# Key parts, score maxima and value biases of a two-layer attention kernel moved between engines and DMA queues

## The reference

```python
x = x + attention0(norm(x), ctx)   # 16 heads of 8, keys and values from ctx, biases bq bk bv bo
x = x + butterfly_ffn(norm(x))     # 128 -> 512 by W_exp and 9 butterfly stages, gelu, 9 stages and W_con back
x = x + attention1(norm(x), ctx)   # the same shape, its own weights
x = x + experts(norm(x))           # sigmoid router, top 4 of 16 experts of width 64, one shared expert
```

## Time and profile before

| | us |
|---|---|
| median of 3 runs | 208.7 |
| the profiled execution | 208.64 |
| its span in the trace | 206.8 |
| PE busy | 197.8 (96%) |
| DVE busy | 151.3 (73%) |
| ACT busy | 146.4 (71%) |
| POOL busy | 57.7 (28%) |
| granted PE clock | 1.00 throughout |

### The profile page before, as it was taken

One profiled execution on the slowest core, in us unless ns is written; L12 is line 12 of the kernel. 1 busy time (PEld: TensorE's weight loads), 2 busy tenths in 40 slices (PEclk: granted clock), 3 DMA queues, 4 the chain that ended last, 5 costly groups with the idle time before them and its releaser, 6 DMA issues.

```text
span 206.8 us, 4279 instructions
## 1 busy us (share of the span) xinstructions
PE 197.8 (96%) x1721; PEld 110.1 (53%) x1728; DVE 151.3 (73%) x240; ACT 146.4 (71%) x264; POOL 57.7 (28%) x74
## 2 busy tenths in 40 slices
...
DMA packets 6084, 10.51 MB, mean 51 GB/s; under 512 B 1152, under 2 KB 3120, under 8 KB 5936
## 3 DMA queue, kind: packets, MB, share of 16 engines
...
...
HBM read 9.64 MB, written 0.59 MB: 49 GB/s over the span
## 4 chain that ended last, share of the span: by engine, by line
PE 84%; ACT 7%; DVE 5%; issue 2%; DVEq 0%; ACTq 0%
PE PS L362 63%; PE OB L362 21%; ACT P L866 3%; DVE T L1009 2%; DVE xn L997 1%; DVE Q L1018 1%; ACT sums L882 1%; ACT Q L837 1%; ACT o_raw L876 1%; ACT sums L885 0%; DVE x L1046 0%; DVE x L1053 0%; DVE sums L1033 0%; DVE attn L1039 0%; ACT K L832 0%
## 5 line engine op out<-in xcount | busy, mean ns | idle before, releaser
L1009 DVE TENSOR_REDUCE T<-PS 128x4 f32<-128x1024 f32 x64 | 76.6, 1220 | 7.7 <-PE PS L362 6.8
L866 ACT ACTIVATE P<-PS 128x512 f32<-128x512 f32 x128 | 68.2, 600 | 15.4 <-PE PS L362 15.3
L362 PE MATMUL OB<-P,V 128*32 128x256 f32 x512 | 33.8, 384 | 0.3
L766 POOL TENSOR_TENSOR attn<-o_raw,sums 128x512 f32<-128x512 f32 x5 | 6.4, 1284 | 91.4 <-ACT sums L885 91.4
L362 PE MATMUL PS<-K,Q 32*128 32x256 f32 x256 | 29.3, 323 | 0.8 <-DVE T L1009 0.3
L362 PEld LDWEIGHTS PS<-K,Q 32*128 32x128 f32 x256 | 18.1, 183 | 19.7 <-DVE T L1009 6.0
L362 PE MATMUL PS<-Q,K 32*128 32x256 f32 x256 | 27.1, 322 | 0.9 <-ACT P L866 0.7
L362 PEld LDWEIGHTS PS<-Q,K 32*128 32x128 f32 x256 | 17.1, 183 | 14.0 <-ACT P L866 7.3
L919 ACT ACTIVATE gate_t<-PS 128x512 f32<-128x512 f32 (+1 forms) x18 | 10.4, 596 | 18.2 <-DVE prod_t L1118 12.1
L362 PEld LDWEIGHTS OB<-P,V 128*32 128x32 f32 x512 | 14.3, 109 | 11.1 <-ACT P L866 1.1
L1118 DVE TENSOR_TENSOR prod_t<-PS,gate_t 128x512 f32<-128x512 f32 x16 | 10.9, 687 | 9.2 <-POOL hid_t L778 7.2
...
## 6 DMA issues: line engine op xcount, KB each, us to landing
spread<-comb_out SPq DMA_DIRECT2D x32, 128.0 KB, 3.0
...
x<-xT SPq DMA_DIRECT2D x2, 128.0 KB, 3.3
cx<-ctxT SPq DMA_DIRECT2D x2, 128.0 KB, 3.5
```

The lines of the kernel that those rows point to most:

```text
L362: return nc.tensor.matmul(out, lhsT, rhs, start=start, stop=stop)
L766: finish(nc.gpsimd.tensor_tensor(attn[:, :, queries(b)], o_raw[:, k % 2, :].rearrange("p (a q) -> p a q", a=2), sums[:, k % 2, :].rearrang ...
L866: finish(nc.scalar.activation(P[:, (JOINT * U + j) % (JOINT * PUNITS), :, :].rearrange("p k q -> p (k q)"), PS[:, FILLED["sc", U, j // 2][ ...
L1009: finish(nc.vector.tensor_reduce(dst, two("max", U, i).rearrange("p j (t s) -> p j t s", t=2), AX.X, ALU.max, negate=True), "red", U, i)
```

## The change

Five things change.

- **Keys by DMA** (`MOVED`): the keys of span (0, 2) (layer 0, batches 2 and 3) and both spans of layer 1 are no longer spread by `ksel` and `kev` (12 steps each). Their weight columns are permuted so that the parts come out row by row; POOL stores high, low and high part to DRAM (`kst`, three DMAs) and reads them back spread (`kld`, four DMAs). The ones come from a constant plane that SP copies into the same DRAM tensor.
- **Maxima by DMA** (`ld`): `turn` and `shift` (17 each) are gone. `red` writes `T` with even and odd queries side by side (`max` takes every second query as stationary column), and SP moves each head's 256 values from 128 partitions into one row of Q, two DMAs behind each `red`, 128 in all. `sc` waits for them.
- **Value biases** are folded through the output weights into the output bias (`fb` on PE, `fbr` on DVE); `vev` becomes a copy, half on ACT, half on DVE.
- **`up` in three float32r passes**: the weights and the normed rows are split into high and low parts (`uhi` on ACT, `ulo` on DVE, one more subtraction in `fwr.3`).
- **Buffers and order**: `P` is four units deep, and all five orders are written anew (a list for SP is new); evictions and copies change engines in some places; the fills grow from 32 to 38 matmuls.

```diff
-PUNITS = 3
+PUNITS = 4
+RING = 8
+MOVED = ((), ((0, 2), (1, 0), (1, 1)))
...
+SP_ORDER = """
+ld.1.0 ld.0.0 ld.0.1 ld.1.1 ld.3.0 ld.3.1 ld.2.0 ld.2.1 ld.4.0 ld.5.1 ld.5.0 ld.4.1 ld.6.1 ld.7.0 ld.6.0 ld.7.1
...
 POOL_ORDER = """
-expand mixdn mixup nmul.0.0 nmul.0.1 nmul.0.2 nmul.1.0 load wsplit nmul.1.2 hid.0.1 hid.0.4 hid.0.5 hid.0.6
-hid.0.7 hid.1.0 hid.1.1 hid.1.4
+expand kst.0.2 mixdn kld.0.2 kst.1.0 mixup nmul.0.0 kld.1.0 nmul.0.2 kst.1.1 load wsplit kld.1.1 nmul.1.0
+nmul.1.1 hid.0.2 hid.0.3 hid.0.5 hid.0.6 hid.1.3 hid.1.5
...
             def maxima(U, i):
...
-                    q0 = b * SEQ + qt * D
+                    half = slice(b * SEQ + qt, (b + 1) * SEQ, 2)
...
-                        last = mm(two("max", U, i)[:, jj, qt * SEQ:(qt + 1) * SEQ], Q[rows, g, q0:q0 + D],
+                        last = mm(two("max", U, i)[:, jj, qt * SEQ:(qt + 1) * SEQ], Q[rows, g, half],
                                   K[l][rows, g, queries(b)])
...
             def scores(U, i):
-                after(pe, "shift", turned_with(U))
+                turned_waited(pe, U, i)
...
+            def three(to, w_high, w_low, high, low, start=True, stop=True):
+                mm(to, w_high, high, start=start, stop=False)
+                mm(to, w_high, low, start=False, stop=False)
+                return mm(to, w_low, high, start=False, stop=stop)
+
+            def fold(*at):
...
+                for l in range(LAYERS):
+                    for a in range(2):
+                        last = mm(bank("fb")[:, l:l + 1], w_o[:, l, a, :], bvc[:, l, a:a + 1], start=a == 0, stop=a == 1)
+                give(last, "fb")
...
-                give(mm(bank("up", c, k), w_up[:, k, :], xn[:, chunk(c)]), "up", c, k)
+                give(three(bank("up", c, k), w_up_hi[:, k, :], w_up_lo[:, k, :], n_hi[:, :], n_lo[:, :]), "up", c, k)
...
         def _(sp):
...
+            def turn(U, i):
+                l, b, g = unit(U)
+                after(sp, "red", U, i)
+                if U >= RING:
+                    turned_waited(sp, U - RING, i)
+                for j in (2 * i, 2 * i + 1):
+                    sp.dma_start(Q[32 * j + g:32 * j + g + 1, g, queries(b)].bitcast(f32), T[:, U, j, :].bitcast(f32))\
+                        .then_inc(turned_in[i][U % RING], 16)
...
         def _(pool):
...
+            def store_parts(kind, l, p):
+                after(pool, "qlo" if kind == 0 else "klo", l, p)
+                if n > 1:
+                    if fresh(pool, stack_in[kind], 64 * (n - 1)):
+                        pool.wait_ge(stack_in[kind], 64 * (n - 1))
...
+                for r, part in enumerate((high, high, low) if kind == 0 else (high, low, high)):
+                    pool.dma_start(part_rows[kind][r + 1], part[:, at].bitcast(f32)).then_inc(parts_out[kind], 16)
+
+            def load_stacks(kind, l, p):
...
+                if fresh(pool, parts_out[kind], 48 * n):
+                    pool.wait_ge(parts_out[kind], 48 * n)
...
+                for j in range(JOINT):
+                    pool.dma_start((Q if kind == 0 else K[l])[32 * j:32 * j + 32, :, lo:hi].bitcast(f32), by_head[:, :, j, :])\
+                        .then_inc(stack_in[kind], 16)
...
             def reduce(U, i):
...
-                dst = T[:, t % TURNS, :, :].rearrange("p t (j r) -> p j t r", r=32)[:, 2 * i:2 * i + 2, :, g]
-                finish(nc.vector.tensor_reduce(dst, two("max", U, i).rearrange("p j (t s) -> p j t s", t=2), AX.X,
+                finish(nc.vector.tensor_reduce(T[:, U, 2 * i:2 * i + 2, :], two("max", U, i).rearrange("p j (t s) -> p j t s", t=2), AX.X,
                                                ALU.max, negate=True), "red", U, i)
-
-            def shift(t):
-                dst = Q[:, g:g + n, queries(b)]
-                filled(dve, "turn", t)
-                finish(nc.vector.tensor_tensor(dst, bank("turn", t)[:, 0:SEQ].unsqueeze(1).broadcast_to([D, n, SEQ]),
-                                               dst.bitcast(f32), ALU.add), "shift", t)
```

More of the change, by code:

```diff
@@ L49 @@
[L49 to L73, removed]
@@ L79 @@
+dn.1.7 dn.1.8
 """
 DVE_ORDER = """
[L81 to L94, removed]
+xcopy.0 normed.0 xcopy.1 klo.0.0 klo.0.1 qlo.0.0 kev.0.0.0 normed.1 kev.0.0.3 red.0.0 qlo.0.1 red.0.1 red.1.0
```

447 lines of the change are left out of this document (282 added, 165 removed).

## The result

The changed kernel takes 208.14 us (median of 20 runs, 205.31 to 212.26), the kernel before 208.70 us beside it (208.17 to 209.09). The ratio is 0.9919, with a 95% interval of 0.9893 to 0.9945; all ratios here leave out the runs that lie over 1.5% above the fastest of the same kernel, here nine of the twenty. The forecast was 198.5 us, with 190 to 207 as the range. The runs of the changed kernel lie apart, and their times go with the mean granted clock of TensorE, as 205.31 us at 0.996, 208.14 at 0.983 and 212.26 at 0.951 show. The profiled execution of the kernel before has 1.0.

A forecast was written before the change was run, and what follows sets the result against it. PE was taken as the bound, with 84% of the chain. Gains of 4.0 us (22.5 to 60 us), 1.3 (60 to 92.4) and 4.8 (92.4 to 152) sum to 10.1: 208.6 to 198.5 us, range 190 to 207.

The forecast's parts named there:

- Turns: `turn` steps on PE: 0.55 us each, 17 removed, 15 of them behind 22.5 us, 8.25 us won.
- key stacks: Key-spreading products on PE: 0.35 us each, twelve removed, eleven behind 22.5 us, 3.85 us won (3.3 to 5.1).
- about 12 us lower: Sign of being right: PE's busy time falls by about 12 us.
- PE work that goes should shorten the end almost one for one: Removed PE work shortens the run nearly fully, if DVE falls too from 22.5 to 60 us and replacements arrive in time.
- Keys through DRAM: Span (0, 2)'s keys, needed by `max.8` at about 37.5 us, land 3.7 us early to 1.4 late; cost taken as 0.
- DMAs of maxima: SP's transfers behind each `red`: landing taken as 3.3 us, covered by 5 us and more of `red`; no later cost.
- Up: Three float32r passes win 0.27 us on each of 8 products, 2.2 us, less 1.6 us for a longer path.
- DMAs land late: Rival: keys and maxima landing after 6.7 us cost 5.4 us, giving 203.9 us (203 to 207.5); chance 0.13.
- the rival on weights: Rival: `max` loading every second column as weights doubles its 0.30 us of loads, 9.6 us in all, 208.1 us; chance 0.07.
- the `max` of unit 8 released by POOL's loads: Sign of being wrong: a `max` of unit 8, 16 or 24 starts only when POOL's loads release it.
- the 2 us named as a sign of being right: Sign of being right: PE's waits for DMAs of `T` absent or under 2 us in sum.
- SP's queue: Rival: 128 DMAs through one queue bind from 1.0 us each; at 1.2 us the time is 222 us; chance 0.10.

The follow-up runs named there:

- the sixth experiment: Changed kernel with keys of span (0, 2) loaded from SP's queue and the experts' load delayed until unit 17's maxima are reduced: 202.13 us, ratio 0.9686.
- The second experiment: Changed kernel with the loads of the keys of span (0, 2) issued by SP behind their stores, not by POOL: 204.98 us, ratio 0.9675.
- the cover: Changed kernel with seven products on zeros before unit 8's first maximum and six more before unit 16's first scores: 206.72 us, ratio 0.9826.
- the seventh experiment: As the sixth experiment, with up in one float32 pass again: 201.37 us, ratio 0.9668.

## Why the prediction was wrong

**The terms of PE's work held, but PE's busy time fell by less.** Turns at 0.55 us and key stacks at 0.35 were not too large (0.68 to 0.80 and 0.37 when added). Counted in the traces from each product's start to the next one's start or its own end, the sixth experiment has 12.7 us less of PE's time in the changed steps: turns 9.8, key stacks 3.8 and `up` 1.6 less, the fold 0.9 and the fills 1.6 more. That agrees with the "about 12 us lower" of the prediction. PE's busy time as a whole is only 9.0 us lower, since products that no edit meant to change take 3.7 us more, 1.4 of them the scores `sc`. So "PE work that goes should shorten the end almost one for one" failed in part. The prices were taken from rows in which the removed products partly run beside others; whether that explains the 3.7 us is not shown.

**"Keys through DRAM ... I take 0" failed.** The mechanism was in the text, its size not. The mixes ended at 31.4 and not at 30.0 us, and the last load took 7.74 us from its issue, beyond the 6.7 I had as the upper end. That bound came from one transfer of 256 KB among others; here four follow each other. `max.8`, expected at 37.5, started at 40.92; PE was there 1.55 us earlier, at 39.4. The second experiment takes this wait away and 3.2 us with it.

**"DMAs of maxima": the landing taken was too long alone and far too short in company.** 2.0 us against my 3.3 where nothing else moves, but 4.8 beside the keys and 4.1 beside the experts' load. The sentence "the lists keep two to four units of `max` ahead of `sc`" holds within a stage and not where layer 1 starts: there only unit 17's maxima stand between those of unit 16 and its scores. Where that distance is kept, 6.5 us beside the bulk cost no more than 0.91 us (sixth experiment). I had named this place in a rival and gave it 1 us; it cost 1.43 and what came behind. The Trainium skill ("DMA: Bandwidth & Descriptors", Anatomy of one DMA) gives about 2 us fixed per DMA for those that GpSimd issues; SP's 2.0 us here agree with it. The same page of the Trainium skill says, under Queues, rings and completion order, that an engine takes packets from its queues in turn. That fits SP's maxima slowing down beside POOL's bulk; no run shows the mechanism. Beside keys on SP's own queue the maxima took 4.2 us as well (sixth experiment, 28 to 36 us).

**No term stood for the clock.** The rows of before have 1.00 everywhere, so the sum took PE's speed as given. At 0.57 for 4 us and 0.55 for 7.5 us PE does at most 5.1 us less work (4 x 0.43 + 7.5 x 0.45, an estimate). The starts of `red` give some 4 us: with the cover units 8 to 10 take 4.53 us in place of 5.81, and units 16 to 19 take 11.44 in place of 12.69 although six products of 0.23 us stand in them. Covering the pauses gave back 1.4 us in the median, since the wait at unit 16 remained and those six were added; taking the waits away gave 6.0 us, clock and waits together. The runs separate the two only so far.

**"Up" was worth nothing.** A product of three passes starts 0.70 us after the one before, as taken (70.71 and 71.41 us in the changed kernel's profile). In the seventh experiment's, four float32 products take 3.63 us from 65.80 on, 0.91 each, so 0.21 us are won per product and not 0.27. And that experiment is not slower without the passes: the gain of 0.6 in the sum was not there.

**What is still missing.** With both waits gone 202.13 is 3.6 us above the forecast. By the page some 3 us of it are PE work that did not fall (9.0 us and not 12), and under 1 us is idle time beyond the 1.6 that the sum had charged (2.4 us more than before). Part of the idle time stands at 84.71, where PE waits 0.92 us for layer 1's first queries. Before, work that is now removed stood there, and no wait did:

```profile
88.74 0.49 PE L362 MATMUL PS<-k_hi,selr 32*128 32x512 f32 x1
...
89.27 0.51 PE L362 MATMUL PS<-q_hi,selr 32*128 32x512 f32 x3
```

I had counted removed work at its full price also where it covered a wait. The new orders, the fourth buffer of P and the fold of the biases were not tested by themselves.

**The rivals.** "DMAs land late" named both places and gave 203 to 207.5; its mechanism was the right one, the clock left out. By the number the rival on weights, 208.1, was nearer still, and that is luck. Of the signs of being wrong the `max` of unit 8 released by POOL's loads came true. PE's waits for maxima, 1.6 us in sum, stayed under the 2 us named as a sign of being right: that sign left out what follows a wait. SP's queue was not the bound of the whole: an issue of a maximum takes 0.60 us and not 0.43, which makes 77 us for 128, and four bulk issues more did it no harm. For a short stretch, 59.5 to 65 us, the chain does run through its issues, one of them of 1.67 us, but PE waits only 0.22 us behind them. Weights at a step of two cost nothing to speak of: four loads of a `max` take 0.31 us, 0.30 before.

```profile
15.16 0.31 PEld L398 LDWEIGHTS PS<-K,Q 32*128 32x128 f32 x4 [0.76 <-DVE T L1143]
```
